# Perceiver block on one Trainium2 core: layer norm and gate of the experts moved into the semilinear stage's last group, rows gathered normalised, softmax sums in PSUM

## The reference

```python
x = x + xattn(ctx, ctx, layernorm(x))        # deformable attention, 16 heads, NK = 5 samples per query
x = x + semilinear(layernorm(x))             # chunks of 16 tokens, two gradient steps per chunk
x = x + ffn(layernorm(x))                    # one of 8 experts per token

def ffn(x, gate_w, expert_w):
    scores = einsum('bsh,eh->bse', x, gate_w)
    onehot = one_hot(argmax(scores, -1))
    return x + einsum('bsef,bse->bsf', einsum('bsh,efh->bsef', x, expert_w), onehot)
```

## Time and profile before

| | |
|---|---|
| median of 3 runs | 1356.28 us (1356.2 to 1358.26) |
| profiled execution | 1352.66 us, its span 1350.9 us |
| busy share of the span | PE 81%, DVE 67%, ACT 37%, POOL 25% |
| mean granted clock of TensorE | 0.894 of full speed |
| end of project (semilinear stage) | 1146.4 us |
| first instruction of routing | 1192.4 us |
| first gather, first expert product | 1214.2 us, 1223.8 us |

### The profile page before, as it was taken

How to read it: one execution, slowest core, us unless ns; L and a number is a source line. 1 busy time by engine, 2 the same in 40 slices (tenths; PEclk the granted TensorE clock), 3 DMA queues, 4 the chain that set the end, 5 groups by cost and what they waited for, 6 DMA issues and landing times. The chain is left out here.

```text
span 1350.9 us, 19405 instructions
## 1 busy us (share of the span) xinstructions
PE 1096.4 (81%) x6220; PEld 788.2 (58%) x6221; DVE 905.4 (67%) x1674; ACT 496.9 (37%) x985; POOL 340.3 (25%) x341
## 2 busy tenths in 40 slices
PE   5984999999999548798989798988889646547886
PEld 5872666656666427686758576766758534333332
DVE  3654689987897726687877759676877643545553
ACT  1221367666677523442434234333424220311110
POOL 1335466766675500000000000000000000004453
PEclk9996988898888568899989899998999877767899
DMA  4364012220110020001000010101000000452221
GB/s 151 130 249 90 22 38 54 52 52 16 37 31 16 16 75 4 32 1 47 1 20 29 2 48 1 48 2 48 1 16 1 1 16 3 143 244 62 74 77 36
DMA packets 54498, 67.14 MB, mean 50 GB/s; under 512 B 37197, under 2 KB 41741, under 8 KB 52369
## 3 DMA queue, kind: packets, MB, share of 16 engines
q1 hardware_dynamic: 48432, 49.31, 11.4%
q0 software_dynamic: 3680, 8.40, 1.9%
q10 hardware_dynamic: 2304, 8.39, 1.6%
HBM read 51.14 MB, written 18.61 MB: 52 GB/s over the span
## 5 line engine op out<-in xcount | busy, mean ns | idle before, releaser
L1141 POOL COPY fw_hx<-fw_hT 128x128 f32<-128x128 f32 x32 | 8.0, 293 | 524.3 <-ACTq L1531 524.3
L539 POOL TENSOR_TENSOR aw_wtent<-aw_tent,aw_e 128x1760 f32<-128x1760 f32 x32 | 100.6, 3145 | 119.5 <-DVE aw_e L535 119.5
L729 PE MATMUL aw_psum_kv<-all_xWv,aw_c 128*128 128x512 f32 x256 | 130.1, 656 | 0.0
L511 POOL TENSOR_TENSOR aw_tent<-all_const,all_ix 128x1760 f32<-128x1760 f32 x32 | 100.6, 3145 | 5.2 <-POOL aw_wtent L539 4.6
L1869 PE MATMUL ex_psum_prod<-ex_We,ex_gT 128*128 x184 | 91.0, 642 | 5.9 <-issue 5.9
L835 ACT ACTIVATE aw_cT<-aw_psum_av 32x256 f32<-32x256 f32 x128 | 80.6, 629 | 39.6 <-PE aw_psum_av L758 38.5
L717 PE MATMUL aw_psum_kv<-aw_c,all_xWk 128*128 128x352 f32 x256 | 81.3, 473 | 9.5 <-POOL aw_A L616 9.5
L729 PEld LDWEIGHTS aw_psum_kv<-all_xWv,aw_c 128*128 128x128 f32 x256 | 51.4, 211 | 56.8 <-issue 55.6
L1558 ACT ACTIVATE fw_at<-fw_at,fw_atop 128x128 f32<-128x128 f32 x128 | 49.5, 388 | 74.6 <-DVE fw_atop L1284 74.6
L522 DVE TENSOR_TENSOR aw_prod<-aw_tent,aw_psum_s 128x1760 f32<-128x1760 f32 x32 | 63.5, 1985 | 17.8 <-ACT aw_tent L517 11.5
L717 PEld LDWEIGHTS aw_psum_kv<-aw_c,all_xWk 128*128 128x128 f32 x256 | 48.9, 195 | 35.1 <-POOL aw_A L616 9.6
(11 more groups left out here) (243 smaller groups left out, 2312.7 us busy)
## 6 DMA issues: line engine op xcount, KB each, us to landing
ex_We<-expert SPq DMA_DIRECT2D x1, 8192.0 KB, 23.6
aw_craw<-ctx SPq DMA_DIRECT2D x8, 704.0 KB, 4.8
pj_x<-x_tok SPq DMA_DIRECT2D x8, 512.0 KB, 3.6
q_scr<-pj_QT ACTq DMA_DIRECT2D x8, 512.0 KB, 2.9
aw_Qb<-q_scr SPq DMA_DIRECT2D x32, 128.0 KB, 3.5
c_scr<-aw_cT ACTq DMA_DIRECT2D x8, 512.0 KB, 2.7
fw_cT<-c_scr SPq DMA_DIRECT2D x8, 512.0 KB, 4.1
fw_x<-x_lb SPq DMA_DIRECT2D x8, 512.0 KB, 5.0
```

The lines of the kernel that those rows point to most:

```text
L511: return nc.gpsimd.tensor_tensor(self.tent[r][:], bc(rows, 1, self.nu * NK), bc(ix, 2, self.wr), ALU.subtract)
L539: return eng.tensor_tensor(self.wtent[:], self.tent[r][:], bc(self.e[:].rearrange("p u k -> p (u k)"), 2, self.wr), ALU.mult)
L729: mm = nc.tensor.matmul(ps_kv[:, j % 2, :], rows, Wv[:, c, :], start=(c == 0), stop=(c == KC - 1))
```

## The change

1. In the attention windows the row maximum, the sum of the exponentials and a partial sum of the samples move to a PSUM bank `small`. `dve_sum_tree` becomes `dve_sum_chain`: four additions of 352 elements, the first of two SBUF tiles into PSUM, two from PSUM and SBUF into PSUM, the last into A.
2. The scratch `x2_scr` becomes `xh_scr`: for each token its row of x and, beside it, its normalised row. In the last round of the semilinear stage SP loads the rows of groups 0 to 6 back into tiles that are free by then; DVE takes statistics (`gate_stats`) and normalises in place (`gate_rows`) in four batches of groups, (0, 1), (2, 3), (4, 5, 6) and (7); PE turns a group (`gate_turn`) and multiplies it with the gate weights (`gate_score`, now with the rows stationary and 8 columns moving), in PSUM banks that the front work has left; ACT takes square roots and copies the turned rows to `hT` (`gate_copy`); SP stores the normalised rows. Groups 4 (its score) to 7 come after `project`. At the end DVE copies all scores to SBUF.
3. `experts_phase` loses the gate loop and begins with routing; `We`'s load is its first DMA. The loop over slots is written out: gathers of 4-KB rows (x and normalised) into a ring of four, with the index column read in place; no norm, no index copy. DVE adds x + h in place (`together`) and the product (`result`).

```diff
-    def dve_sum_tree(self, nc, chain):
+    def dve_sum_chain(self, nc, chain):
 
         part = self.wtent[:].rearrange("p (u k) m -> p u k m", k=NK)
-        n = self.nu * self.wr
-        two = self.prod[:].rearrange("p u m -> p (u m)")[:, 0:2 * n].rearrange("p (u k m) -> p u k m", u=self.nu, k=2)
-        chain.link(nc.vector.tensor_tensor(two, part[:, :, 0:2, :], part[:, :, 2:4, :], ALU.add))
-        chain.link(nc.vector.tensor_tensor(two[:, :, 0, :], two[:, :, 0, :], two[:, :, 1, :], ALU.add))
-        return nc.vector.tensor_tensor(self.A[:, :, 0:self.wr], two[:, :, 0, :], part[:, :, 4, :], ALU.add)
+        chain.link(nc.vector.tensor_tensor(self.acc, part[:, :, 0, :], part[:, :, 1, :], ALU.add))
+        for n in range(2, NK - 1):
+            chain.link(nc.vector.tensor_tensor(self.acc, self.acc, part[:, :, n, :], ALU.add))
+        return nc.vector.tensor_tensor(self.A[:, :, 0:self.wr], self.acc, part[:, :, NK - 1, :], ALU.add)
...
+        rows_in = [f[0]["q"], f[0]["k"], f[0]["v"], xs, h, x1[0], cT]
+        rows_in = [b[:].rearrange("p a n -> p (a n)").rearrange("p (t d) -> p t d", t=TT) for b in rows_in]
+        GATES = ((0, 1), (2, 3), (4, 5, 6), (7,))
+        rows_h = rows_in + [e[0][:]]
+        rows_x = rows_in + [x2[:]]
...
+            def gate_store(g):
+                sp.wait_ge(gh_done.sem, gh_done.at(g, 1))
+                sp.dma_start(a["xh_scr"][g, :, :, 1], rows_h[g]).then_inc(gh_out.sem, 16)
...
+                    sp.wait_ge(*back.full(t.r, "sk0"))
+                    sp.wait_ge(x_out.sem, x_out.at(t.r - 1, 0))
+                    gate_load(0, 0)
+                    gate_load(1, 0)
+                    gate_load(2, 1)
...
+            gate_load(6, 2)
+            for g in range(4):
+                gate_store(g)
...
+            def gate_stats(b):
+
+                if b < 3:
+                    dve.wait_ge(g_in[b].sem, g_in[b].at(len(GATES[b]), 0))
+                ch = Chain(dve, glink, b)
+                tiles = [(g, j) for g in GATES[b] for j in range(TT)]
+                for n, (g, j) in enumerate(tiles):
+                    last = nc.vector.bn_stats(gst[:, n, :], rows_x[g][:, j, :])
+                ch.link(last)
+                for n in range(len(tiles)):
+                    last = nc.vector.bn_aggr(gmv[:, n, :], gst[:, n, :])
+                last.then_inc(gvar.sem, 1)
+
+            def gate_rows(b):
+
+                ch, n = Chain(dve, glink, b), len(GATES[b]) * TT
+                ch.n = 1
+                dve.wait_ge(gstd.sem, gstd.at(b, 1))
+                ch.link(nc.vector.reciprocal(grs[:, 0:n], grs[:, 0:n]))
+                for m_, g in enumerate(GATES[b]):
+                    for j in range(TT):
+                        n = m_ * TT + j
+                        row = nc.vector.tensor_scalar(rows_h[g][:, j, :], rows_x[g][:, j, :], gmv[:, n, 0:1], grs[:, n:n + 1],
+                                                      ALU.subtract, ALU.mult)
+                    row.then_inc(gh_done.sem, 1)
...
                 maxima(i, ch, 0)
+                if last:
+                    gate_stats(0)
                 normalise(t, ch, 0)
                 ahead("q0", "q1", "q2", "q3")
                 step_weights(i, ch, 0)
+                if last:
+                    gate_rows(0)
...
+                    gate_stats(1)
...
+                    gate_rows(1)
...
+            gate_stats(2)
             causal_products(NG, 1)
+            gate_rows(2)
             leave(LAST, NG)
+            gate_stats(3)
+            gate_rows(3)
+            dve.wait_ge(gs_ps.sem, gs_ps.at(NG, 0))
+            nc.vector.tensor_copy(k["scores"], front.ps[:, 3, 0:TILES * E])
...
+            def gate_turn(g):
+
+                pe.wait_ge(gh_done.sem, gh_done.at(g, 1))
+                for j in range(TT):
+                    tile = g * TT + j
+                    if tile >= 3:
+                        pe.wait_ge(gt_cp.sem, gt_cp.at(tile - 3, 1))
+                    for c in range(KC):
+                        last = nc.tensor.transpose(front.ps[:, tile % 3, c * P:(c + 1) * P], rows_h[g][:, j, c * P:(c + 1) * P], k["ident"])
+                    last.then_inc(gt_ps.sem, 1)
+
+            def gate_score(g):
+
+                if g == 0:
+                    pe.wait_ge(wg_in.sem, wg_in.at(0, 16))
+                pe.wait_ge(gt_cp.sem, gt_cp.at(g * TT + TT, 0))
+                for j in range(TT):
+                    at_ = (g * TT + j) * E
+                    for c in range(KC):
+                        mm = nc.tensor.matmul(front.ps[:, 3, at_:at_ + E], hT[:, c, j * P:(j + 1) * P], Wg[:, c, :],
+                                              start=(c == 0), stop=(c == KC - 1))
+                mm.then_inc(gs_ps.sem, 1)
...
                         go("k2", "k3", "v0", "v1")
+                        if last:
+                            gate_turn(0)
+                            gate_score(0)
+                            gate_turn(1)
                 go("v2", "v3")
+                if last:
+                    gate_score(1)
                 pe.wait_ge(w_done.sem, w_done.at(i, 3))
                 blocks(i, back, "sk1", KC, [(key[:, g, halves[1]], win[:, g, :]) for g in by_g])
...
                 transposes(i, back, "wo", [wout[:, g, :] for g in by_g])
+                if last:
+                    gate_turn(2)
+                    gate_score(2)
+                    gate_turn(3)
...
             turned_softmax(LAST, NG, 1)
             causal(NG, 1)
+            gate_score(3)
             output(LAST, NG, 1)
+            gate_turn(4)
             back.skip(pe, NG, *TURN)
             project(NG)
+            gate_score(4)
+            for g in range(5, NG):
+                gate_turn(g)
+                gate_score(g)
...
+            def gather(r):
+                if r >= len(ring):
+                    pool.wait_ge(res_done.sem, res_done.at(r - len(ring), 1))
+                index = bass.IndirectOffsetOnAxis(ap=row[:, r:r + 1], axis=0)
+                nc.gpsimd.indirect_dma_start(xg[r % 4][:].rearrange("p s d -> p (s d)"), None, x_rows, index, bounds_check=B * L - 1,
...
+            def together(r):
+                dve.wait_ge(g_in[r % 4].sem, g_in[r % 4].at(r // 4, 16))
+                nc.vector.tensor_tensor(xg[r % 4][:, 0, :], xg[r % 4][:, 0, :], xg[r % 4][:, 1, :], ALU.add).then_inc(gx_done.sem, 1)
...
+            for r in range(SLOTS):
+                if r + 1 < SLOTS:
+                    turned(r + 1)
+                which = pe.value_load(expert[0:1, r:r + 1], min_val=0, max_val=E - 1)
...
```

More of the change, by code:

```diff
@@ L1599, in group @@
                 exponentials(i, 1)
+                if last:
+                    gate_copy(2)
             deviation(FIRST)
@@ L1610, in _ @@
             end(NG)
+            for g in range(4, NG - 1):
+                gate_copy(g)
+            gate_deviation(3)
+            gate_copy(NG - 1)
 def running_sum(nc, chain, bufs, n):
@@ L1724, in _ @@
-            rounds(pool, SLOTS - 3, tile)
-            for r in range(SLOTS - 3, SLOTS):
-                scatter(Round(r // 2, r % 2))
-            for p in range(2):
+            for r in ring:
+                gather(r)
+            for r in range(SLOTS):
+                if r + len(ring) < SLOTS:
+                    gather(r + len(ring))
+                scatter(r)
+            for p in two:
                 pool.wait_ge(g_out[p].sem, g_out[p].at((SLOTS + 1 - p) // 2, 0))
@@ L1837, in _ @@
-            turned(Round(0, 0))
-            pe.wait_ge(w_in.sem, w_in.at(0, 16))
-            rounds(pe, NG, group)
-            pe.wait_ge(*gate.used(NG - 1, "g"))
-            for t in range(TILES):
-                mm = nc.tensor.transpose(ps_s[:, t * E:(t + 1) * E], scores[:, t, :], k["ident"][0:E, 0:E])
-            mm.then_inc(slot_ps.sem, 1)
             pe.wait_ge(slot_in.sem, slot_in.at(0, 1))
@@ L1862, in tile @@
-            def tile(t, last):
-                if not last:
-                    slots_turned(t.next())
-                which = pe.value_load(expert[0:1, bass.ds(t.r, 1)], min_val=0, max_val=E - 1)
-                pe.wait_ge(*gturn[t.p].used(t.i, "t"))
-                pe.wait_ge(*prod[t.p].free(t.i, "y"))
-                for c in range(KC):
-                    mm = nc.tensor.matmul(prod[t.p].bank("y"), gT[t.p][:, c, :], We[:, bass.ds(which, 1), c, :].rearrange("p o d -> p (o d)"),
-                                          start=(c == 0), stop=(c == KC - 1))
-                mm.then_inc(prod[t.p].filled.sem, 1)
@@ L1878, in _ @@
         @block.scalar
         def _(act):
-            def deviation(t):
-                act_deviation(nc, act, t.r, mv, rstd[:], var, std)
-            def turned(t):
-                for j in range(TT):
-                    act.wait_ge(*turn.full(t.r, f"t{j}"))
-                    nc.scalar.activation(hT[:, :, j, :], turn.bank(f"t{j}", KC), ACT.Copy).then_inc(turn.read["act"].sem, 1)
-            def group(t, last):
-                if not last:
```

(6 more changed lines are left out.)

238 lines of the change are left out of this document (111 added, 127 removed).

## The result

The changed kernel takes 1297.53 us (median of four runs, 1292.32 to 1298.62) where the kernel before took 1356.79 beside it: ratio 0.9554, 95% interval 0.9527 to 0.9581. The prediction was 1309, its range 1293 to 1325. The profiled execution took 1292.32, its span is 1290.5 (before: 1352.66 and 1350.9), so the profiles differ by 60.4 us.

What follows compares the result with a forecast made beforehand. PE, with DVE close behind, was taken to bound the attention windows, and a serial chain everything from 1147 us on. Terms -2, -16.5 and -28.4 sum to -46.9: 1352.66 becomes 1305.8, plus 3.6 gives 1309 us, range 1293 to 1325.

Steps and rivals of the forecast that it cites:

- the forecast's own 1301 to 1316: Whole kernel: range of the main case, 4.0 us a slot and half clock behind project, given 0.55.
- that of the slots: Sign of being right: products of neighbouring slots 3.9 to 4.1 us apart, with no wait on a gather.
- Project's end and routing's start: Signs of being right: project ends at 1153 to 1157, routing starts at 1173 to 1178 us, clock about 0.50.
- two signs of being wrong: After project, a clock of 1.00; in the windows, PE's waits for A gone or grown past 19.8 us.
- Slots: Expert slots: PE sets the pace at 4.0 us a slot, ends 3.88 and 4.5; 93.6 against 118.8, -25.2 us.
- rival 2: Slots: GpSimd sets the pace if 4-KB gathers cost twice the time, 4.63 us a slot, 1324 us; chance 0.17.
- rival 3: Slots: gathers land late; at 6.0 us a slot the gain is lost, 1357 us and more; chance 0.03.
- Last group: Last semilinear group: inserted norm and gate work exceeds the waits it fills, +8.5 us, from 4 to 12.
- Behind project: Project's end to routing: remaining gate work at half clock, 6.2 us a group; 1154.9 to 1175.9, where it took 46.0.
- rival 1: After project: clock stays full, the tail costs 13 in place of 21 us, 1302 or 1299 us; chance 0.2.
- Windows: Attention windows: softmax sums in PSUM leave DVE even, wait moves to the first add; -2 us, between -6 and +3.
- First gather to first product: From POOL's first gather to PE's first expert product: 7.2 against 9.57 us, -2.4.

Runs made afterwards that it cites:

- ring3: The changed kernel with three gather buffers in place of four: 1322.81 us in a single run.
- gate_behind: The changed kernel with all the gate's statistics, rows, turns, scores and copies moved behind project, reloads staying inside the last group: 1327.7 us, ratio 0.9738.
- pool_add: The changed kernel with the first of the four additions of the softmax sums done by GpSimd in place: 1311.06 us, ratio 0.9651.
- lock_free: The changed kernel plus unread dense products, with DVE copying the first sample to PSUM and the sums of pairs 1 and 2 placed earlier: 1290.71 us, ratio 0.9508.

## Why the prediction was right, and where it was 12 us off

1297.5 lies in the range but below the forecast's own 1301 to 1316, and no large error was cancelled by another: four terms came out 2 to 6 us better, two 0.9 worse. Of the signs named, that of the slots came true (3.87, next to 3.9 to 4.1, with no wait on a gather). Project's end and routing's start came 8 and 11 us earlier than their ranges, and two signs of being wrong appeared: full clock behind project, for 7 us, and waits for A past 19.8.

- **Slots, right in kind, -25.2 taken, -28.8 measured.** PE sets the pace, at 3.87: the end of the forecast's 3.88 to 4.5 that came from the one undisturbed pair of slots in the earlier trace rows. The gap of 0.42 in the next row, which I had averaged in, does not occur in the slots after (PE's products have no idle time before them); what made it was not looked into. GpSimd's gathers did not double (rival 2: 1022 ns, not 2.1 us), and ring3 shows how near rival 3 lies: with one buffer less the gathers set the pace, at 5.18.
- **Last group, the term that was mis-sized: +8.5 taken, +2.5 measured (+0.8 against gate_behind).** I had added each inserted step's overhang, what it is longer than the wait it fills. The turned softmax rows come at 1127.14 before and 1126.36 after, with windows that end 3.9 earlier: 3.1 late, where I had +6.8 up to there. Of the 3.1, 2.0 belong to turn 2, score 2 and turn 3 (3.5 taken), and 1.1 to all that is ahead of them (3.3 taken). From there to project's end it takes 0.65 less than before, where I had +1.75: I left out what filled waits do to PE, which idles less, and the turned rows and the causal products take 1.58 and 1.17 for 1.97 and 2.09 (and 1.97 and 2.09 again in gate_behind). Ahead of that the steps were shorter than I had them: statistics cost 0.64 apiece and rows 0.50 when issued in pairs, not 0.691 and 0.544, so the batches of DVE's statistics fit the waits for the exponentials: of 3.25 us 0.5 and 0.7 are left over (1106.37 for the earlier trace rows's 1109.86).
- **Behind project, -25.0 taken, -28.6 measured.** I took half clock for all three groups; it came with the score of the second, so rival 1 held for 7 us. In the eight profiles with this tail 17.4 us pass there four times and 19.8 four times, so 2.4 of the 3.6 are the luck of this execution. The price at half clock was right (6.07 in gate_behind), the point of its onset was not to be read from before.
- **Windows, -2 taken, -3.9 measured, for a wrong reason.** I expected the wait to move to the first addition and DVE to come out even. The subtraction lost its 0.88 a pair, and the first addition waits 0.39, no longer than that of the tree (0.48: its mean of 1364 less the 0.88 that it takes undisturbed). So DVE gained 24 us. PE's waits for A did not fall, they rose by 5.3 us, and the gain is PE's own time, 8.6 us less at a higher clock, a term that the sum did not have. "PE is the limit" was incomplete too: with DVE relieved by 48 us the windows shorten by 28.
- **First gather to first product, -2.4 taken, -1.5 measured.** The second gather takes 5.49 to land, where I had 4.8 for a gather.
- Two rules were weighed. The Trainium skill, "SBUF — State Buffer", section "Who interferes with whom", has a DVE instruction with two SBUF inputs contend with a GpSimd instruction that reads SBUF, and one with a single SBUF input not. The traces agree: 195 ns with one operand in PSUM, 1080 with none; 912 for the first addition although it writes PSUM, 525 for the copy with a single SBUF input. The Trainium skill, "VectorE: DVE Perf Modes", section on the TRN2 errata, gives a PSUM source 120 fixed cycles and an SBUF source 58. The additions with one PSUM source take 532 ns, those of before with two SBUF sources 525: the measurement decides, and PSUM costs nothing to speak of here.

## What to carry to other kernels

Work put into waits of a serial chain can cost less than its overhang where it keeps PE from idling: here 1 to 3 us inside the last group, and 37 us when the same work stood behind it, at half clock. Before a loop's gain is credited to the work that was taken out of it, put the work back in an order that runs ahead; here 20 of 30 us were left, which came with the ring, the in-place index and the written-out loop. Then take the other part away too: with three buffers the whole gain was gone. In a hand-written order an instruction that waits is priced by what stands behind it: the same norm cost 10 us or 65.

## What the runs showed of the hardware that was not expected

- An addition of two SBUF tiles that comes behind a GpSimd operation can take until that one ends: 2.30 us for 0.53 of work in pool_add, and moving one of the additions to GpSimd made it the rule (mean 1577 ns, 25 of 32 stretched).
- Products that nobody reads, put where PE waits, paid: 17 of them, 19 us of PE, took 7 us off the span, since narrow products, transposes and the first dense product behind them ran at the upper clock.
- A busy PE does not by itself keep the clock up: in lock_free it fell to 0.50 in every steady group, and in the 2-us windows at 0.50 PE was busy in 2.00 of 2.
